# Softmax sums by TensorE, node rows from extended weights copied out by ScalarE, in a window-attention and graph-routing kernel

## The reference

```python
# window attention, 8 heads of 16 channels, windows of 8 x 8 pixels (64 tokens), shifted by 4
attn = einsum('bhct,bhcs->bhts', q, k) * 16 ** -0.5 + bias + shift_mask
attn = softmax(attn, axis=-1)
out  = einsum('bhts,bhcs->bhct', attn, v)
x = x + (Wproj @ roll(out) + bproj)              # q, k, v from the layer-normed x

# graph attention over 32768 tokens and 524288 random edges, 4 heads of 4 experts
h = layernorm(x) @ W_gat                         # (tokens, 4, 4)
a_src, a_dst = (h * att_src).sum(-1), (h * att_dst).sum(-1)
alpha = segment_softmax(leaky_relu(a_src[src] + a_dst[dst]), dst)
agg = segment_sum(h[src] * alpha, dst)
# top 2 of 4 experts by agg, each a 128 -> 256 -> 128 feed-forward; x = x + weighted sum
```

## Time and profile before

| | us |
|---|---|
| median of three runs | 8292.23 (8291.91 to 8293.34) |
| the profiled execution | 8293.7 |
| its span, from first to last instruction | 8291.6 |
| DVE busy, share of the span | 3906.0, 47% |
| POOL busy | 4730.4, 57% |
| PE busy | 2933.2, 35% |
| ACT busy | 1884.4, 23% |
| mean granted clock of PE, as a share of the full one | 0.652 |

### The profile page before, as it was taken

How to read it: one execution, slowest core, us unless ns; L and a number is a source line. 1 busy time by engine, 2 the same in 40 slices (tenths; PEclk the granted TensorE clock), 3 DMA queues, 4 the chain that set the end, 5 groups by cost and what they waited for, 6 DMA issues and landing times.

```text
span 8291.6 us, 47516 instructions
## 1 busy us (share of the span) xinstructions
PE 2933.2 (35%) x14234; PEld 1451.6 (18%) x14234; DVE 3906.0 (47%) x4181; ACT 1884.4 (23%) x2801; POOL 4730.4 (57%) x4876
## 2 busy tenths in 40 slices
PE   2556667666322221222222122221212212100578
PEld 2334444443200000101000010010000000000223
DVE  5998888888523332432333333231111211112799
ACT  1334545444212121211212122121111111100000
POOL 0111211111477777777777777777777777776641
PEclk8778888888665665656666566665656656555555
DMA  1000000000122222222222222221111111111455
GB/s 50 20 25 31 30 31 31 25 28 25 56 60 55 69 73 52 70 58 69 55 69 73 52 73 68 57 62 31 40 34 36 40 30 40 33 23 23 144 184 175
DMA packets 284779, 455.28 MB, mean 55 GB/s; under 512 B 121214, under 2 KB 204382, under 8 KB 262366
## 3 DMA queue, kind: packets, MB, share of 16 engines
q1 hardware_dynamic: 134760, 395.02, 13.1%
q0 software_dynamic: 147648, 56.99, 7.0%
q10 hardware_dynamic: 2208, 1.05, 0.0%
HBM read 231.29 MB, written 221.42 MB: 55 GB/s over the span
## 4 chain that ended last, share of the span: by engine, by line
POOL 50%; issue 19%; DVE 3%; PE 1%; DMA 1%; POOLq 0%; ACT 0%; DVEq 0%
POOL gath L1308 49%; PE bank L1550 1%; DVE yo L1523 1%; POOL got L1585 1%; DMA gate_rows<-gate_dram 0%; DMA gate_dram<-turned_gates 0%; DVE fin L1528 0%; DVE s L1484 0%; DVE sc L1459 0%; POOL first L1737 0%; DVE s L1457 0%; DVE sc L1471 0%; DVE sc L1463 0%; DVE sc L1469 0%; DVE sc L1478 0%
## 5 line engine op out<-in xcount | busy, mean ns | idle before, releaser
L1308 POOL DMA_INDIRECT gath<-node_rows,idx x4352 | 4129.0, 949 | 1326.1 <-issue 1326.1
L1261 PE MATMUL bank<-xm,w_s 128*128 128x512 f32 x1024 | 642.3, 772 | 3751.2 <-ACT scratch_i L1282 3738.6
L1217 DVE TENSOR_TENSOR adst_in<-bank,gath 128x256 f32<-128x256 f32 x68 | 53.4, 786 | 2823.9 <-DMA gath<-node_rows,idx 2823.9
L1261 PEld LDWEIGHTS bank<-xm,w_s 128*128 128x128 f32 x1024 | 227.1, 241 | 4150.0 <-ACT scratch_i L1282 4005.7
L1289 ACT ACTIVATE bank<-diff 128x256 f32<-128x256 f32 x68 | 26.3, 387 | 3742.9 <-DVE diff L1234 3742.9
L1035 POOL TENSOR_TENSOR scratch_i<-xc,dst_f 128x480 f32<-128x480 f32 x64 | 86.3, 1348 | 1302.3 <-ACT dst_f L952 1302.3
L1204 DVE TENSOR_SCALAR scratch_i<-bank,b_s 128x512 f32<-128x512 f32 x256 | 190.2, 749 | 916.5 <-PE bank L1268 523.0
L1268 PE MATMUL bank<-scratch_i,w_s 128*128 128x512 f32 x1024 | 539.1, 683 | 193.0 <-ACT scratch_i L1282 116.3
L1550 PE MATMUL bank<-gate_rows,choose 4*128 4x512 f32 x512 | 447.4, 1064 | 60.1 <-DVE yo L1523 50.1
L1282 ACT ACTIVATE scratch_i<-bank,b_s 128x512 f32<-128x512 f32 x512 | 345.3, 683 | 187.8 <-PE bank L1261 187.1
L1585 POOL DMA_INDIRECT got<-edge_rows,end_i x256 | 245.6, 959 | 206.3 <-DVE gates L1511 128.7
(11 more groups left out here) (215 smaller groups left out, 5879.6 us busy)
## 6 DMA issues: line engine op xcount, KB each, us to landing
gath<-node_rows,idx POOLq DMA_INDIRECT x4352
y_dram<-scratch_i SPq DMA_DIRECT2D x64, 1024.0 KB, 4.0
yo<-y_dram SPq DMA_DIRECT2D x64, 1024.0 KB, 5.2
edge_rows<-rows SPq DMA_DIRECT2D x68, 768.0 KB, 3.4
line<-moved SPq DMA_DIRECT2D x21, 2048.0 KB, 7.0
moved<-line SPq DMA_DIRECT2D x20, 2048.0 KB
scratch_i<-in_x SPq DMA_DIRECT2D x64, 256.0 KB, 2.7
x_dram<-x SPq DMA_DIRECT2D x64, 256.0 KB, 2.2
```

The lines of the kernel that those rows point to most:

```text
L1261: e.matmul(bank[:, k % 2, :], w1_s[:, k // 2, P * (k % 2):P * (k % 2) + P], xm[par][:, :], start=True, stop=True).then_inc(up_full, 1)
L1308: e.indirect_dma_start(gath[par][:, j, :], None, node_rows, bass.IndirectOffsetOnAxis(ap=idx[par][:, j:j + 1].bitcast(U32), axis=0)).then_ ...
```

## The change

The probabilities are no longer divided by their sum. PE sums the transposed probabilities with a constant matrix of zeros and ones, `heads`, which gives each head's row sum on the 16 partitions of its channels; ACT forms the reciprocal as the exponential of minus the logarithm; DVE multiplies the attention output with it while it copies it out of PSUM, in place of ACT. `attend` no longer waits for the product of the probabilities but for their exponential.

The weights of the node rows are extended in the setup by 8 columns that hold the weights times the attention vectors, so that the node product gives all 24 values; ACT copies them out at the end of its round, and DVE's three instructions per half go.

On DVE the order becomes: `weigh_attention(0)`, `scores(0)`, slot 0, `weigh_attention(1)`, slot 1, residual adds, `scores(1)`, slot 2, slot 3. The ACT loop over rounds 2 to 7 is unrolled by three. SP waits for the evacuation of the node products. The semaphores of bank 4 count three uses per group, those of bank 5 two (`pt_uses`).

```diff
+    k, v, d = np.arange(P) // L, np.arange(2), np.arange(4 * DK) // DK
+    put("heads", (2 * k[:, None, None] + v[None, :, None] == d[None, None, :]).reshape(P, P))
...
-        wgat_s = sb("wgat_s", [C, GC])
+        wgat_s = sb("wgat_s", [C, ROW])
+        wgat_att = sb("wgat_att", [C, 2, GC])
...
+            d.step(e.tensor_tensor(wgat_att[:, :, :], wgat_s[:, 0:GC].unsqueeze(1).broadcast_to([C, 2, GC]),
+                                   att_s[:, :].rearrange("p (k c) -> p k c", k=2), ALU.mult))
+            d.settle()
+            d.step(e.tensor_reduce(wgat_s[:, GC:ROW], wgat_att[:, :, :].rearrange("c k (h e) -> c (k h) e", e=NE), AX,
+                                   ALU.add))
...
-            def inverse_sum(g):
...
-                e.wait_ge(exp_ready, t * 2 + g + 1 + OPEN)
-                own.step(e.tensor_reduce(row_sum[:, g], prob[g][:, :, :, :], AX, ALU.add))
-                own.settle()
-                own.step(e.reciprocal(row_inv[:, g], row_sum[:, g]))
-                own.settle()
-                pr = prob[g][:, :, :, :].rearrange("p w h s -> p (w h) s")
-                e.tensor_tensor(pr, pr, row_inv[:, g].rearrange("p w h -> p (w h)").unsqueeze(2)
-                                .broadcast_to([P, 32, L]), ALU.mult).then_inc(probs_ready, 1)
-
+            def weigh_attention(g, u):
...
+                wait_full(e, t, u)
+                e.wait_ge(sums_turned, t * 2 + g + 1 + OPEN)
+                e.tensor_tensor(ot[:, 8 * g:8 * g + 8].rearrange("p w i j -> p (w i j)"), bank[:, 6 + u % 2, :],
+                                inv[g][:, :], ALU.mult).then_inc(evac[u % 2], 1)
+
+            weigh_attention(0, 0)
             scores(0)
             if t:
                 sort_slot(d, t, 0)
-            inverse_sum(0)
+            weigh_attention(1, 3)
+            sort_slot(d, t, 1)
             if has_c:
...
-            sort_slot(d, t, 1)
             scores(1)
             sort_slot(d, t, 2)
-            if has_c:
-                for j in range(2):
-
-                    wait_full(e, t, 18 + j)
-                    nd = node[par][:, 4 * j:4 * j + 4, :]
-                    e.tensor_copy(nd[:, :, 0:GC],
-                                  bank[:, 6 + j, 0:4 * GC].rearrange("p (r c) -> p r c", c=GC)).then_inc(evac[j], 1)
...
-            inverse_sum(1)
             sort_slot(d, t, 3)
...
-                e.wait_ge(probs_ready, t * 2 + g - 1 + OPEN)
+                e.wait_ge(exp_ready, t * 2 + g - 1 + OPEN)
...
+                    if wp == 4:
+
+                        heads = con("heads").rearrange("p (v c) -> p v c", v=2)
+                        e.wait_ge(pt_evac[0], pt_uses(t, g, 0) + 2 + OPEN)
+                        for hh in range(2):
+                            for v in range(2):
+                                m = e.matmul(bank[64 * hh:64 * hh + 64, 4, :], heads[:, v, :],
+                                             pt[:, :, hh, 64 * v:64 * v + 64], start=v == 0, stop=v == 1)
+                        m.then_inc(pt_full[0], 1)
...
-                        m = e.matmul(bank[:, 6 + j, GC * r:GC * r + GC], x2[last][:, 4 * j + r, :], wgat_s[:, :],
+                        m = e.matmul(bank[:, 6 + j, ROW * r:ROW * r + ROW], x2[last][:, 4 * j + r, :], wgat_s[:, :],
                                      start=True, stop=True)
...
-            def copy_attention(g, u):
+            def inverse_sums(g):
                 if not has_c:
                     return
-                wait_full(e, t, u)
-                e.activation(ot[:, 8 * g:8 * g + 8], bank[:, 6 + u % 2, :].rearrange(
-                    "p (w i j) -> p w i j", i=WS, j=WS), ACT.Copy).then_inc(evac[u % 2], 1)
+
+                e.wait_ge(pt_full[0], pt_uses(t, g, 0) + 3 + OPEN)
+                e.activation(inv[g][:, :], bank[:, 4, :], ACT.Ln).then_inc(pt_evac[0], 1)
+                e.wait_ge(pt_evac[0], pt_uses(t, g, 0) + 3 + OPEN)
+                e.activation(inv[g][:, :], inv[g][:, :], ACT.Exp, scale=-1.0).then_inc(sums_turned, 1)
...
             copy_transposed(0)
-            copy_attention(0, 0)
+            inverse_sums(0)
...
             copy_transposed(1)
+            inverse_sums(1)
             exponentials(0)
-            copy_attention(1, 3)
...
             exponentials(1)
             if across:
                 turn_act(e, turns, False)
+            if has_c:
+                for j in range(2):
+
+                    wait_full(e, t, 18 + j)
+                    e.wait_ge(strip_saved, t - 3 + OPEN)
+                    e.activation(node[last][:, 4 * j:4 * j + 4, :], bank[:, 6 + j, 0:4 * ROW].rearrange(
+                        "p (r c) -> p r c", c=ROW), ACT.Copy).then_inc(evac[j], 1)
...
+                wait_evac(e, t, 18)
+                wait_evac(e, t, 19)
                 e.wait_ge(xn_done, t * 4 + 4 + OPEN)
-                e.wait_ge(node_done, t * 2 + 2 + OPEN)
```

## The result

| | before | after |
|---|---|---|
| median, four runs each | 8292.07 us (8291.25 to 8293.34) | 8059.78 us (8058.64 to 8062.27) |
| ratio | 1 | 0.972, interval 0.9703 to 0.9737 |
| span of the profiled execution | 8291.6 | 8056.8 |
| DVE busy in the span | 3906.0 | 3627.7 |
| PE busy, mean granted clock | 2933.2, 0.652 | 3009.5, 0.666 |

The kernel is 232 us faster. In the changed kernel line 628 is the first bias add of the scores, from which rounds are counted, 648 the product of attention with the inverse sums, 420 and 421 the sort's exchange, 486 its first step behind the turn, 785 the new sums on PE, 791 the attention products, 895 the node products and 1026 the copy of the node rows on ACT.

What follows compares the result with a forecast made beforehand. DVE's own work was taken to bound rounds 1 to 7 and plain rounds, a ring through DVE, ACT and PE the others. 69.0 + 69.1 + 20.2 + 53.6 - 2.0 = 210; 8293.7 - 210 - 1.5 = 8082 us, range 8010 to 8200.

Steps and rivals of the forecast that it cites:

- rounds 1 to 7: First seven attention rounds, running without DVE gaps before; forecast to stay bound by DVE and gain 69.0 us.
- the ring: Cycle of waits in an attention round, DVE's scores, ACT, PE and back; forecast to set plain rounds at 47.9 us.
- back rounds: Eight rounds from round 8 on, such as 18, where PE turns the keys back; forecast to gain 20.2 us together.
- plain rounds: Eight rounds from round 8 on, such as 19, without key turns; forecast 47.9 us each, 53.6 gained together.
- across rounds: Eight rounds from round 8 on, such as 20, where PE turns the keys; forecast to gain 69.1 us together.
- the first rival: PE gets quicker: clock stays up at round starts, 34 us; halves overlap fully, 32; 8050 or 8017; chance 0.18.
- The group of sums: PE's four new 512-column products per window group, two groups a round; forecast 3.0 us a group, bounds 2.0 and 4.0.
- the factor 0.75: In pricing PE's new products: part of the two output halves' work overlaps, so 8 x 495 ns x 0.75 gives 3.0 us.
- the low start of plain and across rounds: PE's clock at round starts: today's pattern kept, attention taking 7.37 us instead of 5.26 where PE starts low.
- The step that was to hide: On DVE, the sort's second step, put ahead of the residual adds, hides in the wait for the projections.
- The ring eating most of the gain: Rival: groups of 4.0 us or hand-overs 0.5 dearer give 40 to 80 us back, 8122 to 8162; chance 0.22.
- The slower case: Rival: PE reads 512 columns in strided pieces at low clock, 8.5 us a group, total 8320; chance 0.06.

## Why the prediction was right, and where its terms were off

The forecast was 8082, the result 8060; direction, place and most of the mechanism came out: DVE's work bounds rounds 1 to 7, the ring the back rounds and three of the eight plain ones, the gather runs as long as before. The 22 us between are what two errors of opposite sign leave: back and plain rounds gained 39 more than forecast, rounds 1 to 7 and across rounds 14 less, and start and end 0.5 less, 25 in all between the profiled spans. The profiled execution lay 1.5 above its median before and 1.1 below after, which leaves 22. That the time fell near the forecast is in part luck: half of the first rival, the full overlap, came true, and without the 14 us lost elsewhere it would have been some 8046, outside 8050 to 8120.

*The group of sums was sized wrong: 1.77 us, not 3.0.* The step that failed is the factor 0.75. It was the mean of short runs of attention products, carried to products of 512 columns as if part of the halves' work did not overlap, with the order of the halves as the reason. The run with the order changed takes the reason away, the run with one half done three times shows the full overlap, and the attention products overlap as well; the factor held what a short run has once. The lower bound of 2.0 was the better value, and it too was high: its 495 ns count a last end, and records start 429 ns apart. The rule of the Trainium skill beside it ("TensorEngine Tiling (Array Packing)", Theoretical Speedup) allows up to twice the speed for 64 columns or fewer; the trace agrees, with 1.77 us for eight records of 0.43. 1.2 us times two groups, in eight plain and eight back rounds, are 38 us; DVE's own work let the plain rounds keep only part of them.

*The clock.* The forecast kept the low start of plain and across rounds; the rival had the clock stay up. Both are right in part. By the first eight transpositions (1.97 us low, 1.09 high) six of the eight starts into plain rounds are low, as kept; into the across rounds 11 to 29 four of seven are high, and three low behind the 3 us without a releaser. In the back rounds from 18 on there is a gain that neither named, inside the turn. PE's timeline of round 18 after:

```profile
1118.79 0.65 PE L715 MATMUL bank<-cst,key_a 128*128 128x128 f32 x4 [0.48 <-ACT xc L943]
1119.76 0.66 PE L715 MATMUL bank<-cst,key_a 128*128 128x128 f32 x4
...
1137.00 1.04 PE L895 MATMUL bank<-wgat_s,x 128*128 128x24 f32 x8 [0.36 <-ACT k L1016]
```

Before, PE had idled 3.48 us ahead of the turn and did its first pieces in 1.12; now it idles 0.48 and does them in 0.65. From the first transposition to the last node product that is 1138.04 - 1118.79 = 19.25 against 20.9: 1.65 us that the sum carried over unchanged. It also carried round 18's 20.9 to the rounds ahead of it, where it was wrong from the start. Rounds 9, 12 and 15 took 19.2 already before the change; PE's timeline of round 12 before:

```profile
895.16 0.63 PE L724 MATMUL bank<-cst,key_a 128*128 128x128 f32 x4 [0.50 <-ACT xc L939]
...
913.36 1.04 PE L894 MATMUL bank<-wgat_s,x 128*128 128x16 f32 x8 [0.36 <-ACT k L1012]
```

These three take 19.5 to 20.0 now, and the five others 19.2 to 19.8 against 20.7 to 21.8. The Trainium skill ("TensorE: Matmul & The Clock Gate", Part 1) has the clock follow how busy PE was; the granted clock of rounds 8 to 31 went from 0.84 to 0.92 as PE's idle time fell from 473 to 251 us. With both corrections the first four back rounds come to 55.0 - 2.4 - 1.65 = 50.95; they took 50.5 to 51.2. All eight were forecast at 459.0 and took 434.6: this kind of round alone is 24 us better than forecast, 16 of it in the first four. In the last four, 8.4 better, the shorter turn makes up 5.8; the rest wasn't taken apart.

*Plain rounds.* Forecast 47.9, bound by the ring, with 3 us of waiting on DVE. With the group at 1.77 the same sum gives 45.4; measured were 45.35 in five and 47.0 to 47.5 in three. The agreement with the five is chance: there DVE bounds, 0.8 above the 44.6 forecast for its work as its sort grew, and the ring stands 1 us under it. In the three the ring bounds, as forecast, and is longer than the sum by about what the wait of 3.06 to 3.64 us has over the 1.18 of the others; no term was for it. 14.7 us more gained.

*Rounds 1 to 7: 60.7, not 69.0.* What was taken from DVE is as priced; two things ate 8 us of it. DVE now waits up to 1.4 us for the second scores in four of the seven rounds, 4.2 in all with the residual adds, where the forecast had no gaps. And the sort grew from 305.2 to 309.1 us, since more of its steps meet POOL. No term of the forecast was for that; it held the sort's steps for fixed work that can't grow.

*Across rounds: 63.7, not 69.1.* The turn's wait is 7 us, as forecast:

```profile
1239.40 1.23 DVE L486 SCALAR_TENSOR_TENSOR key_b<-key_a 128x1024 f32<-128x1024 f32 x1 [6.94 <-ACT key_a L910]
```

The sort's growth is larger from round 8 on (632.1 to 662.5 us). In across rounds it is 9.6 (252.3 to 261.9), more than the 5.4 that are missing; the group's shorter time and the four high starts should have helped here, and how these add up wasn't taken apart. The forecast's eight gains come out only with each round's own wait, 7.3 to 7.9 us, of which it shows the 7.3 of round 20.

*The step that was to hide, did:* the sort's second step in the wait for the projections. Moving it back costs 72 us, nearly a third of the whole gain; the sum had counted its hiding as free without giving this price.

*The rivals.* The ring eating most of the gain would have needed groups of 4 us or costly hand-overs: the logarithm follows the group after

```profile
1147.13 0.60 ACT L934 ACTIVATE inv<-bank 128x512 f32<-128x512 f32 x1 [2.05 <-PE bank L785]
1147.76 0.63 ACT L936 ACTIVATE inv<-inv 128x512 f32<-128x512 f32 x1
```

and takes 0.60, the exponential 0.63, 1.25 with what lies between, under the 1.5 taken. The slower case, from 8 us a group on, is far: at 5.2 us a group the kernel takes 8203, still under the 8292 of before.

## What to carry to other kernels

A row sum over heads that VectorE makes in three passes over 2048 elements can be one short product on TensorE and one factor in a copy that is made anyway; it pays in full where VectorE bounds, and elsewhere by what the ring then needs. When a product's price is carried from another one, take it from where records start in a long run, not from the mean of a short one: sixteen records of 64 columns read 46 ns each by their row, and start 29 ns apart. And after work has been taken off the busiest engine, look for where its waits have gathered: here fixed filler work put into them gave another 22 us.

## What the runs showed of the hardware

*VectorE and GpSimd hold each other up.* A product of GpSimd beside a sort operation can lengthen that operation from 2.28 to 3.23 to 3.35 us, about one microsecond; in the changed kernel that befell 67 of the 130 steps that met one, and none of the others. The product is itself lengthened: 16 products of 128x512 that met no VectorE instruction before the change took 1.26 us each, and the 58 that met sort steps alone after it 1.73 to 3.33. GpSimd's product over rounds 8 to 31, before and after (mean ns behind the comma):

```profile
L1046 POOL TENSOR_TENSOR x<-xc,dst_f 128x512 f32<-128x512 f32 x48 | 91.3, 1923 | 246.2 <-ACT dst_f L952 246.2
```

```profile
L1057 POOL TENSOR_TENSOR x<-xc,dst_f 128x512 f32<-128x512 f32 x48 | 126.6, 2656 | 224.2 <-ACT dst_f L956 224.2
```

Same product, 0.73 us longer in the mean. The change moved no work of either engine to the other; it moved the sort's steps together behind the second scores, where GpSimd's products fall. The Trainium skill ("GPSIMD Engine Reference", 8. Key points) names VectorE instructions with two SBUF inputs among those that contend; the sort's exchange is one, and the run with POOL's product doubled agrees, with 109 long operations instead of 71.

*Two output halves of 64 rows run side by side* on TensorE, whatever the order: for 512 columns eight records in 1.77 us, sixteen in 3.49, and 5.20 when twelve of sixteen go to one half; for 64 columns a pair every 58 ns.
